# Three small moves in a fused attention and FP4 feed-forward kernel: when a scale chain runs, how a product is cut, when one GpSimd step is released

## The chip, the cores and the metric

The kernel runs on one NeuronCore of a Trainium2 chip. The metric is device time in microseconds (us) of one execution, the median of several runs. Three runs of the kernel before gave 592.62, 592.73 and 593.84 us, so the median is 592.73 us. One more execution was profiled; it took 592.31 us, and its trace spans 590.6 us from the first to the last instruction.

## The reference

`x` is 4 x 2048 x 256 in float32. Every token row is normalised, and the normalised row goes down two paths that meet in a product:

```python
xn = _layernorm(x, axis=-1)
s  = _L0_attn_ref(xn, Wq, bq, Wk, bk, Wv, bv, gamma)   # linear attention: xn + gamma * (value_sum + Q (K V)) / (L + Q sum(K))
g  = _silu(_L0_ffn_ref(xn, w_gate, w_up, w_down))      # silu(gate) * up, then down; every operand in blocks of 16 in FP4
x  = x + s * g
```

`_L0_ffn_ref` takes each operand, activations too, block by block of 16: scale = max|block| / 6, divide, round to the FP4 grid, multiply by the scale. The hidden width is 704, so gate and up together are 1408 wide.

## The kernel before

The 8192 rows are taken in 32 pairs of 128-row tiles, and an iteration `p` works on several pairs at once, a software pipeline written out by hand for each engine. In iteration p, pair p+3 is normalised and split into a float16 high part (ScalarE) and low part (`x_low`, GpSimd, L530), and its block scales are made (`x_scales`); pair p+2 is rounded to the grid (`x_round`); pair p goes through the gate and up matmuls (L1516) and the product with silu (`h_mul`, L1000); the hidden values of pair p-1 are rounded (`h_round`); pair p-2 goes through the down product; pair p-10 gets s * g (`e_half`, called y below, L1059), and pair p-12 the final sum o = y + x on GpSimd (L591). Each of PE (TensorE), DVE (VectorE), ACT (ScalarE), POOL (GpSimd) and SP (the DMA issuer) runs its own list in order, tied to the others by semaphores. Iterations 12 to 27 are two rounds of a hardware loop over batches of eight pairs, in which the values that semaphores are waited for are held in registers; the others are written out. In six of the eight positions of a batch, steps of the attention's small matrix algebra (`attention(j, c)`) lie between those of the list.

An iteration has two halves, j = 0 and j = 1, one for each tile. On VectorE the first half reads: `h_mul(0,0)`, y of columns 0 to 127, statistics of a later pair (L953, L957) and two small reciprocals and maxima (L1021, L1025), `h_mul(0,1)`, y of columns 128 to 255, the block maxima xam (`x_scales` part 0, L964), the two rounding steps xt and xg (`x_round` parts 0 and 1, L980 and L983), the low part of the hidden scales (`parts` 2, L1030, two instructions), the scale xss (part 1, L967), the low part xs2 of an earlier pair's scales (part 3, L974), the first rounding step of the hidden values (`h_round` 0, L1037), the reciprocal xrr (part 2, L971). The second half begins with `h_mul(1,0)`; in it lie `h_round` 1 (L1040), then for each tile two products hq (L1048), high part (semaphore hhiq) and low part (semaphore hloq). Between the pairs of products of tile 0 and tile 1 are `h_mul(1,1)` and a y. The maxima ham (L1007), hss (L1011) and the reciprocal hrr (L1014) end the iteration.

On GpSimd an iteration is: ht (L571, released by hrr of the iteration before), from iteration 12 on the sum o (L591), the small power steps rs and x_shift (L520, L523, released by `h_round` 0), `x_low` (L530), and the division xt of pair p+3 (`x_divide`, L537, released by the last hq). In position i = 3 of a batch a small power step (L576) stands between ht and o. The sum of pair e runs in iteration e+12.

y lives where the attention product s was left by TensorE (L1537): in columns 352 to 479 of the second bank of each of the two double banks of `GU`, 128 columns in each, beside the gate and up results. TensorE may write gate and up of the next half into a double bank when `h_mul` and y have both read it. `gate_up(p, 1, 0)` waits for y of columns 0 to 127 of the first half.

Of the kernel before, what the change touches and what calls it, by code (L numbers as in the profile page):

```python
# [29 lines left out]
P = 128  # L30
D = 256
# [9 lines left out]
CH = I // 2  # L41
# [10 lines left out]
GRING = 9  # L52
# [18 lines left out]
def build(nc, x, Wq, bq, Wk, bk, Wv, bv, gamma, w_gate, w_up, w_down, out):  # L71
# [3 lines left out]
    with ExitStack() as ctx:  # L75
# [10 lines left out]
        GU = ps("GU", [P, 2, 2, 512])  # L86
# [91 lines left out]
        unm = sb("unm", [P, 2])  # L178
# [40 lines left out]
        def wait(eng, name, value):  # L219

            if not (isinstance(value, int) and value <= 0):
                eng.wait_ge(S[name], value)
# [123 lines left out]
        def s_beside(p, j, tail):  # L346

            if tail:
                return False
            on = active(p if j else p - 1, False)  # L350
            return on["e"] and on["m"]
# [5 lines left out]
        def last_halves(j, i):  # L357

            return j == 0 and i == FIRST
# [122 lines left out]
        def _(pool):  # L482
# [75 lines left out]
            def iteration(p, k, b=0, i=-1, tail=False):  # L558
                on = active(p, tail)
                if i == 3:  # L560

                    wait(pool, "gram_d", 2 * b + 2)
                if on["mb"]:

                    u, q = p - 1, (k + 1) % 2
                    wait(pool, "hrr_d", u + 1)
                    wait(pool, "hg_d", u)
                    if isinstance(p, int) and u == 0:

                        pool.wait_ge(S["wgd"], 3)  # L570
                    g.tensor_tensor(paired(ht[:, 0:2 * I]), paired(h[:, q]), spread(hrr[:, q], 4 * CB),  # L571
                                    ALU.mult).then_inc(S["ht_d"], 1)
                last_batch = isinstance(b, int) and b == BATCHES - 1
                if i == 3 and not last_batch:
                    wait(pool, "nrm_d", b + 1)
                    g.tensor_tensor(inv[:, :], nrm[:, :], half[:, :], ALU.pow).then_inc(S["inv_d"], 1)  # L576
                if on["o"] and not (isinstance(p, int) and p - LAGO == PAIRS - 1):
                    e, ko = p - LAGO, (k + LAGO) % 2
                    wait(pool, "y_d", 4 * e + 4)
                    if isinstance(e, int) and e == PAIRS - LAGE:  # L580

                        pool.wait_ge(S["hloq"], 2 * PAIRS)
                    y_ = y_place(e) if isinstance(e, int) and e >= PAIRS - PB else y[:, ko]
                    if at_end(p):
                        pool.wait_ge(*((S["x_mid_in"], 16) if e == PAIRS - PB else (S["xend_in"], 16 * ENDS)))
                        g.tensor_tensor(end_row(p), y_, end_row(p), ALU.add).then_inc(S["o_d"], 1)
                    else:
                        wait(pool, f"xe_in{ko}", 8 * (e - ko) + 16)

                        wait(pool, f"out_d{ko}", 8 * (e - ko) + 16)  # L590
                        g.tensor_tensor(o[:, ko], y_, xe[:, ko], ALU.add).then_inc(S["o_d"], 1)  # L591
                if isinstance(p, int) and p == 0:
                    pool.wait_ge(S["dupd"], 4)
                    x_low(p, k)
                if on["xf"]:
                    if on["mb"]:

                        wait(pool, "hw_d", p)
                    x_rstd(p + 1)
                if on["xa"]:  # L600
                    if on["mb"]:

                        wait(pool, "hloq", 2 * p - 1)
                        x_low(p, k)
                    if on["mb"]:

                        wait(pool, "hloq", 2 * p)
                    else:
                        pool.wait_ge(S["h_d"], 4)
                    x_divide(p, k)  # L610
                if i == 2 and last_batch:
                    wait(pool, "nrm_d", b + 1)
                    g.tensor_tensor(inv[:, :], nrm[:, :], half[:, :], ALU.pow).then_inc(S["inv_d"], 1)
# [326 lines left out]
        def _(dve):  # L940
# [92 lines left out]
            def h_round(p, k, part):  # L1033
# [7 lines left out]
                if part >= 2:  # L1041
# [5 lines left out]
                    for at, scales, done in ((I, hs1, "hhiq"), (0, hs2, "hloq")):  # L1047
                        v.tensor_tensor(paired(hq[:, q, j, at:at + I]), paired(hg[:, j * I:(j + 1) * I]),  # L1048
                                        spread(scales[:, q, j * HB:(j + 1) * HB], HB), ALU.mult).then_inc(S[done], 1)

            def e_half(p, k, j, c, last=False):
                e, q, row = s_place(p, k, j)
                n = 4 * e + 2 * row + c
                wait(dve, "s_d", 4 * e + 4 if last else n + 1)
                wait(dve, "g_d", 2 * e + row + 1)
                if row == 0 and c == 0:

                    wait(dve, "o_d", e - 1)
                v.scalar_tensor_tensor(y[:, q, row * D + c * P:row * D + (c + 1) * P],  # L1059
                                       s_spare(0, 1 - c) if last else s_spare(c), unm[:, 0:1],  # L1060
                                       ring(gring, e, GRING)[:, row, c * P:(c + 1) * P], ALU.mult, ALU.mult).then_inc(S["y_d"], 1)
# [229 lines left out]
            def iteration(p, k, b=0, i=-1, tail=False):  # L1291
                on = active(p, tail)

                def attention(j, c):
                    step = at_step(ANSWERS, ANSWERS_END, b, (i, j, c))
                    if step == "high_low" and not (isinstance(b, int) and b == BATCHES - 1):

                        wait(dve, "y_d", 4 * b * PB)
                    if step:
                        answer(b, step)  # L1300

                if on["m"]:
                    h_mul(p, k, 0, 0, i)
                if s_beside(p, 0, tail):
                    e_half(p, k, 0, 0, last_halves(0, i))
                if s_beside(p, 0, tail) and last_halves(0, i):
                    e_half(p, k, 0, 1, True)
                attention(0, 0)
                own = on["xf"] and not (isinstance(p, int) and p == 0)
                if own:  # L1310
                    x_front(p + 1, 1 - k)
                attention(0, 5)
                if own:

                    wait(dve, "stats", dve_pairs(p + LEADA + 1))
                    wait(dve, "var_e", p + LEADA + 1)
                if on["mb"]:
                    parts(p, k, 0)
                if own:
                    x_var()  # L1320
                if on["mb"]:
                    parts(p, k, 1)
                attention(0, 1)
                if isinstance(p, int) and p == 0:
                    down_weights()
                if on["m"]:
                    h_mul(p, k, 0, 1, i)
                if s_beside(p, 0, tail) and not last_halves(0, i):
                    e_half(p, k, 0, 1)
                attention(0, 4)  # L1330
                if on["e"] and not on["m"]:
                    e_mul(p, k, 0)
                if on["xa"]:
                    x_scales(p, k, 0)
                attention(0, 2)
                if on["xb"]:
                    x_round(p, k, 0)
                    x_round(p, k, 1)
                if on["mb"]:
                    parts(p, k, 2)  # L1340
                if on["xa"]:
                    x_scales(p, k, 1)
                if on["xb"]:
                    x_scales(p - 1, 1 - k, 3)
                attention(0, 3)
                if on["mb"]:
                    h_round(p, k, 0)
                if on["xa"]:
                    x_scales(p, k, 2)
                if on["m"]:  # L1350
                    h_mul(p, k, 1, 0, i)
                if s_beside(p, 1, tail):
                    e_half(p, k, 1, 0)
                if on["xb"]:
                    x_round(p, k, 2)
                if on["mb"]:
                    h_round(p, k, 1)
                attention(1, 0)
                if on["mb"]:
                    h_round(p, k, 2)  # L1360
                if on["m"]:
                    h_mul(p, k, 1, 1, i)
                if s_beside(p, 1, tail):
                    e_half(p, k, 1, 1)
                attention(1, 1)
                if on["mb"]:
                    h_round(p, k, 3)
                if on["m"]:
                    h_scales(p, k, 0)
                if on["e"] and not on["m"]:  # L1370
                    e_mul(p, k, 1)
                attention(1, 2)
                attention(1, 3)
                if on["m"]:
                    h_scales(p, k, 1)
                    h_scales(p, k, 2)
# [419 lines left out]
```

## Time and profile before

| | |
|---|---|
| median of 3 runs | 592.73 us (592.62 to 593.84) |
| profiled execution | 592.31 us |
| its span, first to last instruction | 590.6 us |
| TensorE matmul busy | 547.1 us, 93% |
| TensorE weight load busy | 425.8 us, 72% |
| VectorE busy | 553.9 us, 94%, 1172 instructions |
| ScalarE busy | 420.2 us, 71% |
| GpSimd busy | 252.4 us, 43%, 213 instructions |
| granted TensorE clock, mean | 0.993 of full speed |

A row of a view that lists groups ends with the busy time, the mean duration of one instruction in ns, and the idle time of the engine before them with what ended it. A row of the timeline is one instruction, or several alike in sequence (x2 says two). The duration of an instruction begins while the one before it on the same engine is still draining, by 0.07 to 0.09 us, so two in sequence take less than the sum of their durations. A wait for a semaphore counts as idle time; a wait for a memory port is inside an instruction's duration, since the instruction has been issued.

### The profile page before, as it was taken

The numbers are of one execution on the slowest core, as the hardware profiler recorded it, in microseconds if no ns is written. First come the engines' busy times: TensorE is split into PE (matmuls) and PEld (weight loads), VectorE is DVE, ScalarE is ACT, GpSimd is POOL, SyncE is SP. The second block draws the span as 40 slices with busy tenths as digits, with TensorE's granted clock in tenths as the row PEclk, the third lists the DMA queues.
The fourth block names the chain that finished last, engine by engine and source line by source line (L and its number), as shares of the span: only waits on it lengthen the run. The fifth ranks groups of instructions, "written<-read, shape, count | busy, mean of one in ns | idle before, by whom it ended". The sixth has DMA issues, their size and how long they took to land. (4 is left out here: it accounts for less than half of the span.)

```text
span 590.6 us, 15231 instructions
## 1 busy us (share of the span) xinstructions
PE 547.1 (93%) x4973; PEld 425.8 (72%) x4973; DVE 553.9 (94%) x1172; ACT 420.2 (71%) x916; POOL 252.4 (43%) x213
## 2 busy tenths in 40 slices
PE   0478999999999999999999989999999999999996
PEld 0355667778787777778787757778787777778875
DVE  7998999999999999999999998999999999987783
ACT  5989888877787787767686767777677777654431
POOL 7543433333434435435544343444343554422146
PEclk9999899999999999999999999999999999999999
DMA  8010000000011001111011111110111111004124
GB/s 253 18 36 20 20 19 19 19 19 19 19 37 37 19 1 57 55 55 55 24 48 41 54 58 56 55 39 18 55 54 55 55 37 38 22 32 145 37 90 179
DMA packets 17632, 29.14 MB, mean 49 GB/s; under 512 B 2704, under 2 KB 5136, under 8 KB 17552
## 3 DMA queue, kind: packets, MB, share of 16 engines
q1 hardware_dynamic: 17552, 28.13, 14.6%
q8 instruction: 44, 0.72, 0.5%
q14 instruction: 36, 0.29, 0.2%
HBM read 19.73 MB, written 8.39 MB: 48 GB/s over the span
## 5 line engine op out<-in xcount | busy, mean ns | idle before, releaser
L1516 PE MATMUL GU<-wgu,xqT 128*128 128x352 f16 x1536 | 252.4, 315 | 3.0 <-DVE h L1000 2.6
L1516 PEld LDWEIGHTS GU<-wgu,xqT 128*128 128x128 f16 x1536 | 148.3, 99 | 76.3 <-issue 4.1
L571 POOL TENSOR_TENSOR ht<-h,hrr 128x1408 f32<-128x1408 f32 x32 | 82.9, 2590 | 80.1 <-DVE hrr L1014 78.6
L666 ACT ACTIVATE sil<-GU,wkap 128x352 f32<-128x352 f32 x128 | 70.8, 553 | 55.6 <-PE GU L1516 54.5
L1526 PE MATMUL DS<-wdT,hqT 128*128 128x256 f16 x704 | 87.3, 272 | 0.6 <-ACT hqT L673 0.6
L1000 DVE SCALAR_TENSOR_TENSOR h<-GU,wkap,sil 128x352 f32<-128x352 f32 x128 | 68.6, 536 | 12.2 <-ACT sil L666 8.4
L1048 DVE TENSOR_TENSOR hq<-hg,hs 128x704 f16<-128x704 f16 x128 | 79.1, 658 | 1.0
L530 POOL TENSOR_TENSOR xnat<-xs,xnat 128x510 f16<-128x510 f32 (+1 forms) x32 | 37.0, 1159 | 96.6 <-DVE hq L1048 81.1
L1526 PEld LDWEIGHTS DS<-wdT,hqT 128*128 128x128 f16 x704 | 66.8, 98 | 10.5 <-ACT hqT L673 0.9
L520 POOL TENSOR_TENSOR rs<-ve,half 128x2 f32<-128x2 f32 x32 | 22.9, 716 | 111.4 <-DVE ht L1037 106.6
L702 ACT ACTIVATE gring<-DS,hun 128x256 f32<-128x256 f32 (+1 forms) x64 | 29.8, 466 | 42.2 <-issue 28.5
L673 ACT COPY hqT<-TR 128x768 f16<-128x768 f16 x64 | 50.9, 796 | 8.1 <-PE TR L1478 7.1
L1037 DVE SCALAR_TENSOR_TENSOR ht<-hT,ht 128x1408 f32<-128x1408 f32 x32 | 51.8, 1617 | 1.5 <-ACT hT L715 1.5
L1528 PE MATMUL DS<-wdT,hqT 128*128 128x256 f16 x384 | 52.4, 273 | 0.0
L1040 DVE SCALAR_TENSOR_TENSOR hg<-hT,ht 128x1408 f16<-128x1408 f32 x32 | 51.7, 1617 | 0.0
L1007 DVE TENSOR_REDUCE ham<-h 128x88 f32<-128x1408 f32 x32 | 51.4, 1607 | 0.0
L1478 PE MATMUL TR<-id,hq 128*128 128x128 f16 x704 | 50.4, 221 | 1.1 <-DVE hq L1048 0.5
L1537 PE MATMUL GU<-Mx,xnT 128*128 128x128 f16 (+1 forms) x552 | 48.1, 223 | 0.2 <-DVE y L1059 0.2
L1537 PEld LDWEIGHTS GU<-Mx,xnT 128*128 (+1 forms) x552 | 39.5, 98 | 10.6 <-issue 1.0
L537 POOL TENSOR_TENSOR xt<-xs,xrr 128x512 f32<-128x512 f32 x32 | 34.7, 1083 | 27.9 <-DVE hq L1048 25.1
L1478 PEld LDWEIGHTS TR<-id,hq 128*128 128x128 f16 x704 | 43.2, 99 | 4.5 <-issue 1.9
L715 ACT ACTIVATE hT<-ht 128x1408 f32<-128x1408 f32 x32 | 43.8, 1367 | 1.9 <-POOL ht L571 1.3
(185 smaller groups left out, 969.0 us busy)
## 6 DMA issues: line engine op xcount, KB each, us to landing
xin<-in_L_attn_x SPq DMA_DIRECT2D x34, 256.0 KB, 2.9
xe<-in_L_attn_x SPq DMA_DIRECT2D x24, 256.0 KB, 2.8
out<-o SPq DMA_DIRECT2D x24, 256.0 KB, 2.0
algebra<-in_L_ffn_w_down SPq DMA_DIRECT2D x1, 704.0 KB, 6.7
gring<-in_L_ffn_w_up SPq DMA_DIRECT2D x1, 640.0 KB, 5.1
xs<-in_L_attn_x SPq DMA_DIRECT2D x2, 256.0 KB, 4.3
xt<-in_L_attn_x SPq DMA_DIRECT2D x2, 256.0 KB, 4.8
out<-xin SPq DMA_DIRECT2D x2, 256.0 KB, 2.0
```

Source lines behind the costliest of these rows:

```text
L571: g.tensor_tensor(paired(ht[:, 0:2 * I]), paired(h[:, q]), spread(hrr[:, q], 4 * CB), ALU.mult).then_inc(S["ht_d"], 1)
L666: a.activation(sil[:, c], GU[:, c, 0, 0:CH], ACT.Silu, scale=wkap[:, 0:1]).then_inc(S["sil_d"], 1)
L1000: v.scalar_tensor_tensor(h[:, k, (2 * j + c) * CH:(2 * j + c + 1) * CH], GU[:, c, 1, 0:CH], wkap[:, 0:1], sil[:, c], ALU.mult, ALU.mult).t ...
L1007: v.tensor_reduce(per_block(ham[:, :]), paired_in_order(h[:, q]), AX.X, ALU.max, apply_absolute_value=True).then_inc(S["ham_d"], 1)
L1037: v.scalar_tensor_tensor(ht[:, 0:2 * I], hT[:, 0:2 * I], CUT, ht[:, 0:2 * I], ALU.max, ALU.subtract).then_inc(S["hw_d"], 1)
L1040: v.scalar_tensor_tensor(hg[:, 0:2 * I], hT[:, 0:2 * I], CUT, ht[:, 0:2 * I], ALU.max, ALU.subtract).then_inc(S["hg_d"], 1)
L1048: v.tensor_tensor(paired(hq[:, q, j, at:at + I]), paired(hg[:, j * I:(j + 1) * I]), spread(scales[:, q, j * HB:(j + 1) * HB], HB), ALU.mul ...
L1478: last = t.transpose(TR[:, bank, zz * P:(zz + 1) * P], hq[:, q, j, z * P:(z + 1) * P], id16[:, :])
L1516: last = t.matmul(GU[:, c, m, 0:CH], xqT[:, k, j, 2 * a_ + kc], wgu[:, b_, kc, 2 * m + c], start=(z == 0 and kc == 0), stop=(z == 2 and kc ...
L1526: t.matmul(DS[:, 0:D], hqT[:, j, z], wdT[:, z], start=(z == 0), stop=False)
L1528: last = t.matmul(DS[:, 0:D], hqT[:, j, LOCH + z], wdT[:, NCH + z], start=False, stop=(z == LOCH))
L1537: last = t.matmul(bank, slot[:, j, 2 * a_ + kc], Mb[:, b_, kc, columns], start=(i == 0 and kc == 0), stop=(i == 2 and kc == KD - 1))
```

## The change

It has four parts.

- `x_low` on GpSimd waits for the first of the two products hq of tile 0 (`hhiq`) instead of the second (`hloq`).
- y of the first half (j = 0) is one instruction over 256 columns in two banks (`e_row`), at the place where the second of the two stood. The first of them is gone from its place after `h_mul(0,0)`. It raises its semaphore by 2 at its end. One iteration of each batch (`last_halves`) keeps the two.
- Where GpSimd has a sum o to make (`on["o"]`, iterations 12 on), the two rounding steps of `x_round` stand after the scale steps instead of before them.
- There, the reciprocal xrr stands before `h_round` 0 instead of after it, and `parts` 2 after the scale steps.

```diff
                     if on["mb"]:
-                        wait(pool, "hloq", 2 * p - 1)
+                        wait(pool, "hhiq", 2 * p - 1)
                         x_low(p, k)
...
+            def e_row(p, k, j):
+                e, q, row = s_place(p, k, j)
+                halves = lambda ap: ap.rearrange("p (c n) -> p c n", c=2)
+                wait(dve, "s_d", 4 * e + 2 * row + 2)
+                wait(dve, "g_d", 2 * e + row + 1)
+                v.scalar_tensor_tensor(halves(y[:, q, row * D:(row + 1) * D]), GU[:, :, 1, CH:CH + P], unm[:, 0:1],
+                                       halves(ring(gring, e, GRING)[:, row]), ALU.mult, ALU.mult).then_inc(S["y_d"], 2)
...
                 if on["m"]:
                     h_mul(p, k, 0, 0, i)
-                if s_beside(p, 0, tail):
-                    e_half(p, k, 0, 0, last_halves(0, i))
                 if s_beside(p, 0, tail) and last_halves(0, i):
+                    e_half(p, k, 0, 0, True)
                     e_half(p, k, 0, 1, True)
...
                 if s_beside(p, 0, tail) and not last_halves(0, i):
-                    e_half(p, k, 0, 1)
+                    e_row(p, k, 0)
...
                     x_scales(p, k, 0)
                 attention(0, 2)
-                if on["xb"]:
+                if on["xb"] and not on["o"]:
                     x_round(p, k, 0)
                     x_round(p, k, 1)
-                if on["mb"]:
+                if on["mb"] and not on["o"]:
                     parts(p, k, 2)
                 if on["xa"]:
                     x_scales(p, k, 1)
                 if on["xb"]:
                     x_scales(p - 1, 1 - k, 3)
+                if on["xa"] and on["o"]:
+                    x_scales(p, k, 2)
+                if on["mb"] and on["o"]:
+                    parts(p, k, 2)
+                if on["xb"] and on["o"]:
+                    x_round(p, k, 0)
+                    x_round(p, k, 1)
                 attention(0, 3)
                 if on["mb"]:
                     h_round(p, k, 0)
-                if on["xa"]:
+                if on["xa"] and not on["o"]:
                     x_scales(p, k, 2)
```

## Rows read from the trace of the kernel before

**Rows 1.** VectorE's waits from 197 to 524 us: us in total, times, longest.

```profile
DVE h L1000 <- POOL ht L571: 2.8, 1, 2.8
```

**Rows 2.** VectorE's waits over the whole span, the longest in total.

```profile
DVE h L1000 <- ACT sil L666: 8.4, 6, 2.2
```

**Rows 3.** Timeline of VectorE at the end of iteration 16, inside the hardware loop.

```profile
298.94 0.96 DVE L1048 TENSOR_TENSOR hq<-hg,hs 128x704 f16<-128x704 f16 x2
...
300.31 0.34 DVE L1059 SCALAR_TENSOR_TENSOR y<-GU,unm,gring 128x128 f32<-128x128 f32 x1
300.57 1.61 DVE L1048 TENSOR_TENSOR hq<-hg,hs 128x704 f16<-128x704 f16 x2
```

**Rows 4.** Timeline of GpSimd in the same stretch.

```profile
300.21 1.16 POOL L530 TENSOR_TENSOR xnat<-xs,xnat 128x510 f32 x1 [3.12 <-DVE hq L1048]
```

**Rows 5.** All hq products: ns min/median/max, first and last start in us.

```profile
L1048 DVE TENSOR_TENSOR hq<-hg,hs x128: 509/519/1208, 61.5 to 573.8; 128x704 f16<-128x704 f16 x128
```

**Rows 6.** Timeline of VectorE at the end of iteration 1, before the loop.

```profile
61.46 0.96 DVE L1048 TENSOR_TENSOR hq<-hg,hs 128x704 f16<-128x704 f16 x2
...
62.83 1.63 DVE L1048 TENSOR_TENSOR hq<-hg,hs 128x704 f16<-128x704 f16 x2
```

**Rows 7.** Timeline of GpSimd in the same stretch.

```profile
62.49 1.16 POOL L530 TENSOR_TENSOR xnat<-xs,xnat 128x510 f16<-128x510 f32 x1 [2.89 <-DVE hq L1048]
```

**Rows 8.** Timeline of VectorE, iteration 16, the first rounding step.

```profile
291.35 0.68 DVE L980 SCALAR_TENSOR_TENSOR xt<-xT,xt 128x512 f32<-128x512 f32 x1
```

**Rows 9.** Timeline of GpSimd there: the sum o.

```profile
291.77 1.39 POOL L591 TENSOR_TENSOR o<-y,xe 128x512 f32<-128x512 f32 x1
```

**Rows 10.** Timeline of VectorE, iteration 19: xam to the first `h_mul` of half 1.

```profile
342.83 0.67 DVE L964 TENSOR_REDUCE xam<-xs 128x32 f32<-128x512 f32 x1
343.43 1.28 DVE L980 SCALAR_TENSOR_TENSOR xt<-xT,xt 128x512 f32<-128x512 f32 x1
...
345.36 0.43 DVE L1030 SCALAR_TENSOR_TENSOR hs<-hss,hbq,hs 128x44 f16<-128x44 f32 x2
...
345.89 1.62 DVE L1037 SCALAR_TENSOR_TENSOR ht<-hT,ht 128x1408 f32<-128x1408 f32 x1
347.43 0.34 DVE L971 RECIPROCAL xrr<-xss 128x32 f32<-128x32 f32 x1
347.69 0.48 DVE L1000 SCALAR_TENSOR_TENSOR h<-GU,wkap,sil 128x352 f32<-128x352 f32 x1
```

**Rows 11.** Timeline of GpSimd there.

```profile
342.88 1.28 POOL L591 TENSOR_TENSOR o<-y,xe 128x512 f32<-128x512 f32 x1
```

**Rows 12.** The two rounding steps over the span: ns min/median/max.

```profile
L980 DVE SCALAR_TENSOR_TENSOR xt<-xT,xt x32: 679/682/1374, 30.1 to 512.8; 128x512 f32<-128x512 f32 x32
L983 DVE SCALAR_TENSOR_TENSOR xg<-xT,xt x32: 691/692/1650, 30.9 to 513.6; 128x512 f16<-128x512 f32 x32
```

**Rows 13.** The small hidden-scale step from 520 to 560 us: ns min/median/max.

```profile
L1030 DVE SCALAR_TENSOR_TENSOR hs<-hss,hbq,hs x4: 252/258/361, 529.7 to 547.1; 128x44 f16<-128x44 f32 x4
```

**Rows 14.** Timeline of GpSimd at the first of these four.

```profile
528.69 1.27 POOL L591 TENSOR_TENSOR o<-y,xe 128x512 f32<-128x512 f32 x1
```

**Rows 15.** s * g over 256 columns from one bank, grouped by form.

```profile
L1092 DVE SCALAR_TENSOR_TENSOR y<-GU,unm,gring 128x256 f32<-128x256 f32 x6 | 2.8, 479 | 0.3 <-PE GU L1537 0.3
```

**Rows 16.** Timeline of TensorE's weight loads, iteration 19: the gate and up of half 1.

```profile
340.97 1.61 PEld L1516 LDWEIGHTS GU<-wgu,xqT 128*128 128x128 f16 x12 [0.37 <-DVE y L1059]
```

**Rows 17.** Timeline of VectorE there: the second `h_mul` of half 0.

```profile
342.07 0.58 DVE L1000 SCALAR_TENSOR_TENSOR h<-GU,wkap,sil 128x352 f32<-128x352 f32 x1
```

**Rows 18.** Timeline of ScalarE: silu for `h_mul(1,0)` of iterations 19 and 17.

```profile
344.64 0.54 ACT L666 ACTIVATE sil<-GU,wkap 128x352 f32<-128x352 f32 x1
...
311.63 0.56 ACT L666 ACTIVATE sil<-GU,wkap 128x352 f32<-128x352 f32 x1 [1.76 <-PE GU L1516]
```

**Rows 19.** Timeline of VectorE: that `h_mul(1,0)` of iteration 17, and one of iteration 30.

```profile
312.98 0.48 DVE L1000 SCALAR_TENSOR_TENSOR h<-GU,wkap,sil 128x352 f32<-128x352 f32 x1
...
528.34 0.58 DVE L1000 SCALAR_TENSOR_TENSOR h<-GU,wkap,sil 128x352 f32<-128x352 f32 x1 [0.68 <-ACT sil L666]
```

## The prediction

> **What bounds the kernel now.** I read the waits first. From 197 to 524 us, iterations 11 to 29, VectorE waits for another engine once, 2.8 us [rows 1], at the turn of the hardware loop. Over the whole span its largest wait is for silu, 8.4 us in six places [rows 2]; these lie in iterations 0, 1, 30 and 31. So VectorE's own list sets the time in the middle, and a microsecond taken off it there is a microsecond, until TensorE or ScalarE is late. In iterations 8 and 9 silu comes only just in time, and from iteration 30 on TensorE has a part in the pace: in iteration 30 `h_mul` waits for silu [rows 19].
>
> A list can be full and still hold waiting. The timeline shows where. In iteration 16 the first two products hq take 0.96 us together, the next two 1.61 us [rows 3], and one alone has a median of 0.52 us but a maximum of 1.21 us [rows 5]. The long one stands beside `x_low` on GpSimd, 300.21 to 301.37 us [rows 4]. It ends 0.38 us after `x_low`, which is its 0.52 us less some 0.14 us of start: it waited inside itself. The same shows at the first rounding step: 1.28 us [rows 10] beside the sum o, which ends at 344.16 [rows 11], against a median of 0.68 [rows 12]. So a VectorE operation with two inputs in SBUF and a large GpSimd operation exclude each other. The one that is under way goes first: the rounding step at 291.35 kept its 0.68 us [rows 8] although o came at 291.77, and o took 1.39 instead of 1.28 us [rows 9, 11]. It overlapped the running step for 0.26 us and paid 0.11, so again some 0.15 us of an overlap is free.
>
> **x_low one operation sooner.** In the loop `x_low` starts 0.31 us after the second product of tile 0 ends (298.94 + 0.96 = 299.90; 300.21) [rows 3, 4]. The first ends 0.96 - 0.52 = 0.44 us before the second. Released by it, with the same 0.31 us, `x_low` starts at 299.77, beside the last 0.13 us of the second product, which is within the free 0.15. It ends at 300.93 instead of 301.37. The blocked product of tile 1, which starts at 300.57 as before, gets free 0.44 us sooner; 0.2 us of its 0.65 us (1.61 - 0.96) stay. VectorE gains 0.44 us in each of iterations 12 to 27, 16 x 0.44 = 7.0 us.
> Outside the loop `x_low` starts 0.07 us after its release [rows 6, 7]. It will start at 62.05, 0.37 us before the running product ends at 62.42, pay 0.37 - 0.15 = 0.22, and end at 63.43 instead of 63.65: 0.22 us gained. That holds in iterations 1 to 11 and 28. From about 4 to 9 I take TensorE's own list to set the pace (silu has no time in hand at 8 and 9), and what VectorE gains after iteration 28 starts its second half is lost in the wait of iteration 30. I count six, 1.3 us. GpSimd itself has over a microsecond idle ahead of `x_low` in each of these [rows 4, 7], and the step before it, x_shift, is long done.
> The bounds of this part: 0 if the lock behaves otherwise, 12 x 0.22 + 16 x 0.65 = 13 us if nothing of the blocked time stayed.
>
> **y of the first half in one operation.** A y of 128 columns adds 0.26 us to the list (300.31 to 300.57) [rows 3]. One of 256 columns lasts 0.48 us [rows 15] against 0.34, so it adds 0.26 + 0.14 = 0.40. 2 x 0.26 - 0.40 = 0.12 us less in each of 19 iterations, at most 2.3 us. Where o blocks the next step this only makes VectorE arrive sooner and wait longer, so in about half of them it is nothing.
> The price is on TensorE. Its gate and up of the second half is released by the first y now, 340.97 [rows 16]; after the change by `e_row`, which in iteration 19 would end at 342.07 + 0.50 + 0.48 = 343.05 [rows 15, 17]: 2.1 us later. Behind it in TensorE's list are s, the hidden transposes and all later gate and up. Silu for this half starts at 344.64 now [rows 18], about 2 us after the last weight load, since ScalarE is busy with other steps. With gate and up done near 345.0 it starts near 345.1 and ends near 345.7, and `h_mul(1,0)` comes at 347.69 [rows 10]: covered by 2 us. The like lag, worked out in the same way, is 0.5 to 2.2 us in iterations 11 to 14, 19, 20, 22, 27 and 28, 12.1 us together; in 15 to 17 and 23 to 25 TensorE is behind anyway and comes after the place of `e_row`. The lag lasts until TensorE's next wait for VectorE. I take 0.2 us as lost; if the cover were gone everywhere it would be the 12.1 us.
>
> **The scale steps ahead of the rounding.** In iterations 12, 13, 15, 19, 21, 23 and 27 the first rounding step waits some 0.6 us for o, as in iteration 19; in 16, 24, 28 and 29 the second waits some 0.95 us (1.65 against 0.69) [rows 12]. What takes their place right after xam? xss (one input), then xs2, a step with two SBUF inputs like the rounding. It starts where xt started: 0.12 later for xss (0.03 of gap and 0.09 of lost overlap, since xss needs xam finished), 0.1 for xss itself, 0.12 to 0.13 earlier by `e_row`, so 0.1 later. The nearest row for such a small step beside o is that of iteration 30: 361 ns instead of 256 [rows 13], beside an o that ends at 529.96 [rows 14], 0.06 us before it. So it waits too. Then after the end of o there is still all of the old work but xss: 2.0 us before (xt 0.55, xg 0.73, hs2 with xss and xs2 0.53 (345.36 to 345.89), xrr 0.26 (347.43 to 347.69)) [rows 10], 1.9 after. The gain is 0.1 us in the seven, not 0.6. In 16 and 24 hs2 would now wait for o, and both rounding steps come behind it: 0.1 lost each. In 17 and 25, where 0.15 us was lost to o, 0.1 gained. Where nothing collides the order costs the 0.12 us behind xam, which `e_row` pays (14, 20, 22) or not (18, 26: 0.1 lost each). Sum with `e_row` of iteration 11: 0.7 - 0.2 + 0.2 - 0.2 + 0.1 = 0.6. Its bounds: below, -0.12 x 17 = -2 us; above, if small steps slip past o, 7 x 0.5 + 4 x 0.2 = 4.4 us more.
> The reciprocal and hs2 move past no queue but VectorE's; the only reader of xrr, the division on GpSimd, waits for the last hq anyway. ScalarE's input of hs2 was ready before (it is made ahead of its Abs step).
> The Trainium skill, page "SBUF — State Buffer", section "Who interferes with whom", says that a VectorE instruction with two SBUF inputs contends with a GpSimd one that reads SBUF, whichever issued first blocking the other. That speaks against the reordering: xs2 and hs2 have two. The rows above agree for the long steps and, by one row, for the short. It adds tensor_scalar in its two-port modes, which would block xss too; no row here shows it, and it would make the 0.1 of the seven iterations 0.
>
> **The sum.** 7.0 + 1.3 - 0.2 + 0.6 = 8.7 us, of which I take 8.5 for what drains and waits eat. The profiled execution took 592.31 us for its 590.6, so 583.8 against its own time; the median is 0.4 above it: 584.2 us.
>
> **Rivals.**
> Small steps slip past o (0.15): for it, xss and xrr have one input and the row for hs2 is single; against it, that row. 584.2 - 4.4 = 580.
> TensorE or ScalarE takes over (0.18): in iteration 17 silu ends at 312.19 and `h_mul(1,0)` starts at 312.98 [rows 18, 19], so only 0.8 us is in hand there after two or three gains of 0.44. If iterations 15 to 18 and 23 to 26 gave nothing, 8 x 0.44 = 3.5 is lost: 588.
> No change (0.09): two thirds of the lags of `e_row`, 8 us, reach VectorE: 592.2. For it, TensorE has little idle time; against it, the covers above.
> Slower (0.08): `x_low`, now arriving while a product runs, takes the port first. Then the second product of tile 0 waits for all of `x_low` and ends at 301.3 instead of 299.90, and the list is 1.4 - 0.65 = 0.75 us longer each time: 28 x 0.75 = 21 us, or with the rest 605. It decides as soon as a GpSimd operation can pass a running VectorE one; the step at 291.35 speaks against it [rows 8]. Milder, the whole of `e_row`'s lag, 12.1 - 8.5: 596.3.
> The forecast itself has 0.50, with 582.5 to 586.5 as its own range.
>
> **How the numbers follow.** A measurement of this kernel can tell some 0.2%, 1.2 us, from no change. Faster: forecast, first and second rival, 0.83. Same 0.09, slower 0.08. The range reaches from 579.5 (small steps slip past) to 590.0 (TensorE takes over, with something of the lag).
>
> **What would show it.** `x_low` 0.4 us earlier after the first product in the loop; the third hq at 0.7 to 0.75 us there and near 0.98 outside instead of 1.2; the y of 256 columns at 0.48; xs2 or hs2 at about 0.7 us where o overlaps them, and both rounding steps at 0.68 in iteration 19. The gate and up of half 1 starts after `e_row` in iteration 19. The prediction is wrong if new waits of `h_mul` for silu appear in iterations 11 to 29, or if xs2 keeps 0.18 us beside o.

## The result, and the profile after

The changed kernel takes 588.44 us (median of 6 runs, 587.57 to 590.46) beside 593.29 us for the kernel before in the same session (6 runs): ratio 0.9926, 95% interval 0.9902 to 0.9950, so 4.4 us less by the ratio and 4.85 us by the medians. Forecast were 584.2 us, 8.5 us less. The profiled execution took 587.87 us, its trace spans 586.1 us.

Three rows of the page (the hq products beside rows 5). VectorE (DVE) is busy 543.2 us, 10.7 us less than before, and the kernel gained less than half of that:

```profile
PE 541.6 (92%) x4973; PEld 423.6 (72%) x4973; DVE 543.2 (93%) x1153; ACT 421.4 (72%) x916; POOL 245.9 (42%) x213
...
L1000 DVE SCALAR_TENSOR_TENSOR h<-GU,wkap,sil 128x352 f32<-128x352 f32 x128 | 70.5, 551 | 16.7 <-ACT sil L666 13.3
...
L1048 DVE TENSOR_TENSOR hq<-hg,hs 128x704 f16<-128x704 f16 x128 | 69.5, 583 | 1.0
```

The hq products answer to the forecast (0.7 to 0.75 us for the blocked one in the loop, near 0.98 outside: 0.72 to 0.75 and 0.98 to 0.99). Timeline of VectorE at the end of iteration 16 (as rows 3) and of iteration 1 (as rows 6):

```profile
297.64 0.96 DVE L1048 TENSOR_TENSOR hq<-hg,hs 128x704 f16<-128x704 f16 x2
...
299.27 1.17 DVE L1048 TENSOR_TENSOR hq<-hg,hs 128x704 f16<-128x704 f16 x2
```

```profile
62.09 0.96 DVE L1048 TENSOR_TENSOR hq<-hg,hs 128x704 f16<-128x704 f16 x2
...
63.46 1.42 DVE L1048 TENSOR_TENSOR hq<-hg,hs 128x704 f16<-128x704 f16 x2
```

and of GpSimd in both places (as rows 4 and 7):

```profile
298.47 1.16 POOL L530 TENSOR_TENSOR xnat<-xs,xnat 128x510 f32 x1 [2.35 <-DVE hq L1048]
```

```profile
62.69 1.38 POOL L530 TENSOR_TENSOR xnat<-xs,xnat 128x510 f16<-128x510 f32 x1 [2.46 <-DVE hq L1048]
```

In the loop the second pair takes 1.17 us instead of 1.61, in iteration 1 1.42 instead of 1.63, and there `x_low` pays 0.22 us for coming while a product runs (1.38 against 1.16).

What is new is in the waits, and it is what the prediction named as the sign of being wrong: `h_mul` waits for silu in iterations 11 to 29. VectorE, from 190 to 524 us (as rows 1; us in total, times, longest):

```profile
DVE h L1000 <- ACT sil L666: 5.3, 7, 1.7
DVE h L1000 <- POOL ht L571: 2.8, 1, 2.8
```

Of the 5.3 us 1.7 are iteration 30's, whose wait was 0.68 before (rows 19); 3.7 us have come in iterations 14, 15, 23 and 29, where there was none. TensorE's weight loads from 190 to 524 us, the first two groups by time:

```profile
PEld GU L1530 <- DVE y L1056: 3.9, 3, 1.8
PEld GU L1530 <- DVE y L1067: 2.7, 1, 2.7
```

L1056 is `e_row`. Of its nineteen instructions four are waited for: those of iterations 19 and 27 (1.81 us each) and 20 (0.33 us) make up this row, and that of iteration 11 (1.68 us) is put down to issue, though the load starts 0.1 us after `e_row` ends. The 2.7 us of the second row lie at the turn of the hardware loop, where TensorE waits in every trace here, 3.1 us in that of the kernel before. Timeline of the weight loads, iteration 11, and iteration 19 (as rows 16):

```profile
205.09 0.64 PEld L1542 LDWEIGHTS DS<-wdT,hqT 128*128 128x128 f16 x6
207.41 1.62 PEld L1530 LDWEIGHTS GU<-wgu,xqT 128*128 128x128 f16 x12 [1.68 <-issue]
```

```profile
340.52 0.71 PEld L1530 LDWEIGHTS GU<-wgu,xqT 128*128 128x128 f16 x6 [1.81 <-DVE y L1056]
```

And the sum o. Timeline of VectorE in iteration 19 after the change (as rows 10), then GpSimd (as rows 11):

```profile
340.38 0.67 DVE L964 TENSOR_REDUCE xam<-xs 128x32 f32<-128x512 f32 x1
341.09 0.77 DVE L967 TENSOR_SCALAR xss<-xam 128x32 f32<-128x32 f32 x1
341.78 0.18 DVE L974 SCALAR_TENSOR_TENSOR xs<-xss,xs 128x32 f16<-128x32 f32 x1
341.89 0.35 DVE L971 RECIPROCAL xrr<-xss 128x32 f32<-128x32 f32 x1
342.16 0.34 DVE L1030 SCALAR_TENSOR_TENSOR hs<-hss,hbq,hs 128x44 f16<-128x44 f32 x2
342.42 0.69 DVE L980 SCALAR_TENSOR_TENSOR xt<-xT,xt 128x512 f32<-128x512 f32 x1
```

```profile
340.55 1.27 POOL L591 TENSOR_TENSOR o<-y,xe 128x512 f32<-128x512 f32 x1
```

The rounding no longer waits; xss does, 0.77 us where it takes 0.18 alone, until o ends at 341.82. In iteration 16 it is hs2 that waits (1.45 us for the two instead of 0.43):

```profile
290.06 0.35 DVE L971 RECIPROCAL xrr<-xss 128x32 f32<-128x32 f32 x1
290.33 1.45 DVE L1030 SCALAR_TENSOR_TENSOR hs<-hss,hbq,hs 128x44 f16<-128x44 f32 x2
291.71 0.68 DVE L980 SCALAR_TENSOR_TENSOR xt<-xT,xt 128x512 f32<-128x512 f32 x1
```

So the open question was not where VectorE's time went but what took it back. **Theory A:** the wait that the late `e_row` puts on TensorE, handed on from iteration to iteration, since TensorE has no idle time in which to make it good, until silu is late. **Theory B:** TensorE's own work is the bound of iterations 12 to 16, and any faster VectorE would have met it.

### The profile page after: what moved, and what is told of

The parts are those of the page before. It is cut to its first block, busy times and chain, and to the rows that moved or that the text cites. A ratio compares the mean times of both kernels' runs of the same rounds, so it can differ in the third digit from the quotient of the medians.

```text
span 586.1 us, 15165 instructions
## 1 busy us (share of the span) xinstructions
PE 541.6 (92%) x4973; PEld 423.6 (72%) x4973; DVE 543.2 (93%) x1153; ACT 421.4 (72%) x916; POOL 245.9 (42%) x213
## 4 chain that ended last, share of the span: by engine, by line
PE 74%; DVE 12%; issue 6%; ACT 4%; POOL 2%; DMA 1%; SPq 0%; DVEq 0%; ACTq 0%; POOLq 0%
PE GU L1530 32%; PE DS L1540 11%; PE GU L1551 6%; PE DS L1542 6%; PE TR L1492 6%; PE G L1600 4%; PE TR L1508 2%; DVE hg L1040 2%; PE TR L1432 2%; DVE ham L1007 2%; DVE hq L1048 1%; DVE h L1000 1%; PE G L1615 1%; PE G L1641 1%; DMA gring<-in_L_ffn_w_up 1%
## 5 line engine op out<-in xcount | busy, mean ns | idle before, releaser
L1000 DVE SCALAR_TENSOR_TENSOR h<-GU,wkap,sil 128x352 f32<-128x352 f32 x128 | 70.5, 551 | 16.7 <-ACT sil L666 13.3
L530 POOL TENSOR_TENSOR xnat<-xs,xnat 128x510 f16<-128x510 f32 (+1 forms) x32 | 39.6, 1238 | 90.7 <-DVE hq L1048 81.9
L1048 DVE TENSOR_TENSOR hq<-hg,hs 128x704 f16<-128x704 f16 x128 | 69.5, 583 | 1.0
L675 ACT COPY hqT<-TR 128x640 f16<-128x640 f16 x64 | 45.0, 702 | 0.0
```

The source lines that it names most:

```text
L1000: v.scalar_tensor_tensor(h[:, k, (2 * j + c) * CH:(2 * j + c + 1) * CH], GU[:, c, 1, 0:CH], wkap[:, 0:1], sil[:, c], ALU.mult, ALU.mult).t ...
```

## The experiments

e1 to e4 were timed beside the kernel before in one session, e5 to e8 in another on another chip; the kernel before took 592.42 and 592.46 us there. A time is a median; the ratio goes by all runs of a session, and the two can differ by some 0.6 us where the runs of a kernel scatter, as those of e3 to e5 do (586.5 to 589.2 us).

**e1: x_low alone.** The edit against the kernel before:

```diff
-                        wait(pool, "hloq", 2 * p - 1)
+                        wait(pool, "hhiq", 2 * p - 1)
```

> The kernel before with the one edit on GpSimd: x_low released by the first product hq of tile 0. Theory A (the lag that the 256-column y puts on TensorE took the missing gain): without that y TensorE keeps its lead, VectorE's 0.44 us in each loop iteration come through, and the time is 8.0 us under the kernel before, near 585.0 us beside its 593.3; silu waits between 197 and 524 us under 1 us in total. Theory B (TensorE's own work is the bound in iterations 12 to 16, whoever releases it): the same 588.4 us as the changed kernel, silu waits of 4 to 5 us in that stretch, in iterations 15 and 23.

584.72 us, ratio 0.9875 (0.9860 to 0.9890): 7.7 us faster than before, and 3.6 us faster than e4 below (3.0 us by the ratios). VectorE's waits from 190 to 524 us:

```profile
DVE h L1000 <- issue: 3.2, 3, 2.5
...
DVE h L1000 <- ACT sil L666: 0.7, 1, 0.7
```

The 3.2 us are the turn of the loop, 2.5 us, and 0.37 us each in iterations 14 and 22, which the kernel before has too. The 0.7 us is the wait of iteration 30 (rows 19), which now falls into this stretch. Theory B had the same 588.4 us here; it falls. TensorE's weight loads in iteration 11 of e1 go on without a break:

```profile
204.72 0.64 PEld L1528 LDWEIGHTS DS<-wdT,hqT 128*128 128x128 f16 x6
205.37 1.70 PEld L1516 LDWEIGHTS GU<-wgu,xqT 128*128 128x128 f16 x12
```

**e2: the changed kernel without the 256-column y.** Against the changed kernel:

```diff
+                if s_beside(p, 0, tail):
+                    e_half(p, k, 0, 0, last_halves(0, i))
                 if s_beside(p, 0, tail) and last_halves(0, i):
-                    e_half(p, k, 0, 0, True)
                     e_half(p, k, 0, 1, True)
...
-                    e_row(p, k, 0)
+                    e_half(p, k, 0, 1)
```

> The changed kernel with y of the first half in two operations at their old places; x_low and the order as changed. Theory A: 1.5 to 3 us faster than the changed kernel, 585.5 to 587 us, with the waits for silu in iterations 15 and 23 (0.9 and 0.7 us for the second h_mul there now) gone. Theory B: within 0.7 us of the changed kernel, 588 to 589 us, since the waits stay.

586.58 us, ratio 0.9902 (0.9887 to 0.9917), inside A's range though near its slow end. The waits in 15 and 23 are gone, but it is 1.9 us slower than e1, from which it differs by the new order alone: the order costs (1.6 us by the ratios).

**e3: the changed kernel with the old order** (the guards `and not on["o"]` and the second block with `on["o"]` taken out).

> The changed kernel with the old order of scale steps and rounding; x_low and the 256-column y as changed. The trace after shows the wait for the sum o moved from the rounding steps to xss (0.77 us instead of 0.18), hs2 and xs2 and as long as before, so both theories expect the same: 588.4 us, within 1 us of the changed kernel. If the order is worth more than that, the time is 590 us or more.

587.28 us, ratio 0.9911 (0.9897 to 0.9926). The changed kernel was timed in a session of its own; in the ratio, the one measure that the sessions share, e3 is 0.0015 under it, with intervals that overlap: no difference that this measurement can tell. Why the order doesn't show beside the late y was not tested; that VectorE waits for silu there anyway would explain it.

**e4: two y of 128 columns, both at the late place**, with `x_low` as changed and the old order. The y against the changed kernel:

```diff
                 if s_beside(p, 0, tail) and not last_halves(0, i):
-                    e_row(p, k, 0)
+                    e_half(p, k, 0, 0)
+                    e_half(p, k, 0, 1)
```

> x_low as changed, old order, and y of the first half in its two old operations, but both at the late place, after the second h_mul: the lag of TensorE without the shorter y. Theory A: the loss comes with the place, so 588.5 to 590 us, the changed kernel or a little slower (19 x 0.12 us more on VectorE, where it has no waits). Theory B: as e1, 588.4 us; the two theories are told apart by e1 against e4, which A has 3.5 to 5 us apart and B under 1 us.

588.33 us, ratio 0.9926 (0.9912 to 0.9939), within 0.2 us of A's range, and 3.6 us from e1 (3.0 by the ratios) where B had them together. The loss is there with two instructions of the old length: it is the place of the first y, not its form.

**e5: the 256-column y in one position of eight.** `joined` chooses `e_row`; elsewhere the two `e_half` stand at their old places. Against the kernel before, `x_low` left out:

```diff
-                if s_beside(p, 0, tail):
+                joined = i == 6
+                if s_beside(p, 0, tail) and not joined:
                     e_half(p, k, 0, 0, last_halves(0, i))
...
-                    e_half(p, k, 0, 1)
+                    if joined:
+                        e_row(p, k, 0)
+                    else:
+                        e_half(p, k, 0, 1)
```

> x_low as changed, old order, and the 256-column y in position i = 6 of a batch alone (iterations 11, 19 and 27), the two old ones everywhere else. In the trace after, TensorE waits for the 256-column y 1.7 to 1.8 us in these three iterations and runs back to back from there to iteration 15 or 23, 2.0 us later than in e1 all the way. If one such wait per batch is the whole cause, this kernel loses nearly all that e3 and e4 lose: 587.3 to 588.5 us, with waits for silu in iterations 15 and 23. If each late y adds its own part, three of nineteen cost little: 585 to 585.7 us.

588.68 us, ratio 0.9926 (0.9911 to 0.9940), 0.2 us past the expected range: three late y lose as much as nineteen. TensorE's weight loads in iteration 11, and VectorE in iteration 15, 64 us later:

```profile
204.86 0.64 PEld L1540 LDWEIGHTS DS<-wdT,hqT 128*128 128x128 f16 x6
207.19 0.87 PEld L1528 LDWEIGHTS GU<-wgu,xqT 128*128 128x128 f16 x7 [1.68 <-issue]
```

```profile
271.06 0.58 DVE L1000 SCALAR_TENSOR_TENSOR h<-GU,wkap,sil 128x352 f32<-128x352 f32 x1 [0.79 <-ACT sil L666]
...
276.84 0.58 DVE L1000 SCALAR_TENSOR_TENSOR h<-GU,wkap,sil 128x352 f32<-128x352 f32 x1 [0.36 <-ACT sil L666]
```

The y of iterations 12 to 15 stand in their old places here, and VectorE waits all the same: 1.68 us of idle TensorE in iteration 11 come out as 0.79 + 0.36 us of idle VectorE in iteration 15. In the changed kernel the same two waits are 0.94 and 0.39 us.

**e6: the 256-column y where TensorE comes late anyway**, `joined = i in (2, 3, 4)`.

> The complement where TensorE comes late anyway: x_low as changed, old order, the 256-column y in positions i = 2, 3 and 4 alone (iterations 15 to 17, 23 to 25, 31), where in e1 its gate and up of the second half starts 1.4 to 2.7 us after the second h_mul, past the end of the 256-column y. No new wait on TensorE; VectorE has 6 x 0.12 = 0.7 us less to do, of which what falls in iterations 17 and 25 is lost to silu: 584.0 to 584.8 us, e1 or up to 0.5 us faster. If the 256-column y costs anything besides its place, it is 586 us or more.

584.89 us, ratio 0.9871 (0.9857 to 0.9885), 0.1 us past the expected range: e1 and e6 cannot be told apart. Where the gate and up starts after the place of `e_row` anyway, the 256-column y costs nothing, and its gain is too small to see.

**e7: the 256-column y alone**, GpSimd and order as before.

> The kernel before with the 256-column y alone, GpSimd and the order as before. VectorE is shorter by some 17 x 0.12 = 2.0 us. If the place costs only what exceeds silu's cover, then with VectorE slower by 0.44 us an iteration than in e3 the cover at iterations 15 and 23 is near 1.1 us against a lag of 1.9, and 0.8 us is lost per batch, some at 29: within 0.8 us of the kernel before, 591.8 to 593.2. If the lag reaches VectorE whole, 595 us and more; if it were free, 590.4.

592.28 us, ratio 0.9995 (0.9984 to 1.0005): no change. Its waits for silu between 190 and 524 us, all up to iteration 29, are 1.9 us, against 3.7 in the changed kernel up to there. With a slower VectorE silu's cover, the time from its end to its `h_mul`, is wider.

**e8: the order alone.**

> The kernel before with the new order alone. The order moves the wait for the sum o from the rounding to xss and adds the drain between xam and xss: from e2 against e1 +0.15 us in iterations without a collision, +0.2 in iterations 16, 18, 24 and 26, +0.03 in the others, 1.2 to 1.9 us in total: 593.6 to 594.4 us beside 592.4. If the order pays on its own as it was costed in the prediction, 592.0 us.

594.15 us, ratio 1.0026 (1.0016 to 1.0036): 1.7 us slower (1.5 by the ratio). Its xss, and that of the kernel before, ns min/median/max:

```profile
L967 DVE TENSOR_SCALAR xss<-xam x29: 171/180/750, 46.0 to 498.5; 128x32 f32<-128x32 f32 x29
```

```profile
L967 DVE TENSOR_SCALAR xss<-xam x29: 166/173/176, 46.1 to 499.9; 128x32 f32<-128x32 f32 x29
```

**Where each kernel is ahead.** From the timelines: the start of `h_mul(0,0)` of an iteration, less that of the kernel before, in us, both counted from iteration 1 (which takes out differences of -0.06 to 0.63 us that arise before it); the last column is the end of the span.

| iteration | 7 | 8 | 12 | 15 | 16 | 20 | 23 | 24 | 29 | 31 | end |
|---|---|---|---|---|---|---|---|---|---|---|---|
| e1 x_low alone | -1.29 | -0.67 | -1.09 | -2.42 | -2.85 | -4.58 | -5.86 | -6.30 | -7.97 | -7.94 | -7.95 |
| e2 x_low, order | -1.28 | -0.67 | -1.07 | -2.17 | -2.57 | -3.88 | -4.46 | -4.88 | -6.46 | -6.33 | -6.33 |
| changed kernel | -1.29 | -0.68 | -1.22 | -2.63 | -2.13 | -3.38 | -4.93 | -4.70 | -6.26 | -5.05 | -5.05 |
| e3 x_low, wide y | -1.30 | -0.68 | -1.22 | -2.73 | -2.12 | -3.80 | -4.26 | -3.68 | -5.29 | -4.16 | -4.16 |
| e5 wide y at i = 6 | -1.33 | -0.69 | -1.24 | -2.75 | -2.14 | -3.77 | -4.21 | -3.62 | -5.19 | -4.05 | -4.06 |
| e8 order alone | 0.00 | -0.02 | -0.02 | 0.17 | 0.20 | 0.31 | 1.02 | 1.03 | 1.34 | 1.44 | 1.44 |

Read the row of e1: 0.22 us an iteration to the seventh, 0.6 us given back in iteration 7 to TensorE, then 0.42 to 0.45 us in most iterations of the loop. The rows with the late y go with it to 15, or up to 0.3 us ahead; all three lose 0.5 to 0.6 us in iteration 15 where e1 gains 0.43, and 1.1 to 1.2 us in 29 and 30 together. In 23 the changed kernel loses 0.2 us, e3 and e5 0.6, and these two also 0.4 in 22. They agree within 0.11 us in every column.

**TensorE's clock at the turn of the loop.** The wait of iteration 22 is in the traces of e3, e4 and e5, 1.0 to 1.2 us, and not in that of the changed kernel. TensorE's granted clock differs. The stretches around its start after the turn, in e3 and in the changed kernel (the number after the five engines is the granted clock; a row has no engine names, and they stand in the order PE, PEld, DVE, ACT, POOL):

```profile
347.40:350.40 3.00, 1.00 (x6) 0.27 (x4) 2.97 (x7) 0.47 (x1) 1.79 (x2) 1.00 0.03 8
350.40:354.40 4.00, 4.00 (x28) 3.00 (x29) 2.85 (x4) 2.41 (x5) 1.99 (x2) 0.65 0.03 8
```

```profile
348.00:351.00 3.00, 0.75 (x5) 0.14 (x4) 2.97 (x7) 0.57 (x2) 1.15 (x1) 1.00 0.01 3
351.00:355.00 4.00, 4.00 (x38) 2.97 (x39) 2.59 (x4) 3.52 (x7) 2.24 (x2) 1.00 0.03 8
```

In e3 the clock is at the lower of its two levels (1.2 of 2.4 GHz) for most of 4 us, and 28 matmuls are done instead of 38. From the first half's gate and up to the second's, iteration 20 takes 9.6 us instead of 7.9. The traces of the kernel before, e2, e4, e5 and e8 have this, those of the changed kernel, e1, e6 and e7 do not have it there; TensorE was nearly idle before it in all of them (e1: 0.61 us busy of the last 3, full clock after). Where the y is not late VectorE had the time in hand: e2 has no wait in 22. Beside the late y its 1.7 us come on top of the lag:

```profile
391.32 0.58 DVE L1000 SCALAR_TENSOR_TENSOR h<-GU,wkap,sil 128x352 f32<-128x352 f32 x1 [1.17 <-ACT sil L666]
```

is e3 in iteration 22. The runs' times fit this, though they are few. A run with a mean granted clock of 0.999 or 1.0 has no such stretch, since one takes 0.0024 off the mean (0.35 x 4 of 587 us): these took 586.58 and 587.28 us for e3 and 587.12 for e4, against 584.64 for e1. Runs at 0.993 and 0.994 took 588.0 to 589.2 us for e4 and e5. Runs at 0.997 have one such stretch, and only a trace tells where. The changed kernel is less clear: its three runs at 0.999 took 587.57, 587.83 and 589.01 us.

## Why the prediction was wrong

**x_low: right, in mechanism and size.** The forecast for this edit was 7.0 + 1.3 = 8.3 us; e1 measures 7.7 (7.4 by the ratio, 7.95 in the table). In the loop 1.61 - 1.17 = 0.44 us were gained as worked out, outside 1.63 - 1.42 = 0.21 for 0.22, and the price of 0.22 us for an arrival during a running product is the row's 1.38 - 1.16. The iterations outside the loop came to 1.1 us at iteration 12 (the table), and 28 adds 0.2: the 1.3 that was put. The loop brings 6.7 us for 7.0: iterations 17 and 25 gain only 0.17 and 0.15 us, as silu has nothing in hand any more there, and 19 gains 0.71, as the wait at the turn of the loop is 0.28 us shorter (2.50 for 2.78), a wait that is 2.50 to 2.80 us in the ten traces. The rival in which GpSimd passes a running product is excluded by the same rows.

**The 256-column y: the step that failed.** The prediction had the lag of TensorE right (2.1 us in iteration 19; the weight loads start at 340.52, 0.06 us after `e_row` ends at 340.46, and 1.81 us idle) and set it against silu's time in hand at the next `h_mul`: "covered by 2 us". There it was covered. But it also wrote that the lag lasts until TensorE's next wait for VectorE, and did not look for that wait. In e1 it comes in the second half of iteration 15, 0.76 us; with the late y it is gone, used up by the lag. From iteration 11 to there TensorE's gate and up keep their distance to e1, 1.6 us counted as in the table (1.8 to 2.0 us from the start of the traces), with no idle time to make it good. The lag has to be held against the thinnest cover on that way. Silu and its `h_mul` in e1, of the two of iteration 15 that wait in e5 and in the changed kernel:

```profile
268.76 0.56 ACT L666 ACTIVATE sil<-GU,wkap 128x352 f32<-128x352 f32 x1 [0.83 <-PE GU L1516]
...
274.53 0.55 ACT L666 ACTIVATE sil<-GU,wkap 128x352 f32<-128x352 f32 x1 [1.22 <-PE GU L1516]
```

```profile
270.44 0.58 DVE L1000 SCALAR_TENSOR_TENSOR h<-GU,wkap,sil 128x352 f32<-128x352 f32 x1
...
276.05 0.48 DVE L1000 SCALAR_TENSOR_TENSOR h<-GU,wkap,sil 128x352 f32<-128x352 f32 x1
```

Silu ends 1.1 and 1.0 us before them, less than the lag. So a term of 0.2 us for lost cover measured 2.6 us (e3 against e1) to 4.0 us (e5 against e1) by the medians, 2.1 to 3.0 by the ratios; in the three runs without the lower clock it is 1.9 to 2.6 us, and where that clock meets the lag, the wait of iteration 22 comes on top. The reckoning of lags one by one, 12.1 us together, was the wrong shape: the late y of iterations 11, 19 and 27 give the whole loss, as e5 shows, and those after them fall into their shadow. This was the rival "TensorE or ScalarE takes over", whose 588 us is what was measured, but its reason was another: it named the 0.8 us in hand at iteration 17, with the gains of `x_low` alone as the cause, and in e1 that cost only some 0.3 us each time. That its number fits is luck.
That the two edits work against each other shows in the sums: the y alone changes nothing (e7, -0.2 us), `x_low` alone brings 7.7, together 5.1 (e3). A faster VectorE uses up the cover that the lag needs.

**The order: the wait moved as predicted, its cost was missed.** Forecast was that a small step with two SBUF inputs waits for o, so that the reordering saves nothing of the 0.6 us. That held: hs2 waits in iteration 16. What the sum missed is that xss, with one input, waits too; the prediction had no row for it and named it only as a possibility, with this result. With it the 0.1 us gained in seven iterations is 0.0, and e2 lies 0.02 to 0.05 us behind e1 in each of 12, 13, 15, 21 and 23. The drain between xam and xss, put at 0.12 us, measured 0.14 to 0.16 where nothing collides (14, 18, 22, 26), and the 0.1 us lost in 16 and 24 was 0.19. Iterations 19 and 20 add 0.8 us between e2 and e1. 0.23 of it is the wait at the turn, 2.74 us against 2.50, which varies from trace to trace (2.52 in e8) and can't be laid to the order. In iteration 20 e2 and e8 both lose 0.5 us: the 0.15 behind xam, 0.29 us for which VectorE stands idle before xrr, put down to issue, which neither e1 nor the changed kernel has, and the overlap lost with it. Why it stands there is open. Together 1.7 us (e8) to 1.9 us (e2 against e1) are lost by the medians. The 0.6 us of the prediction was for the order and the shorter y together: 0.12 of it is iteration 11's, and 0.36 is what the shorter y pays in iterations 14, 20 and 22, so 0.1 us was put for the order alone. In the changed kernel the loss does not show in the time (e3).
The rule of the Trainium skill, "SBUF — State Buffer", "Who interferes with whom", that a tensor_scalar in a two-port mode contends with GpSimd, agrees with the trace: xss takes 0.77 us instead of 0.18 beside o. The trace shows the wait, not the mode.

**The sum.** 8.3 + 0.6 - 0.2 = 8.7 was written and taken as 8.5. The measured pieces by the medians are 7.7 for `x_low`, -2.6 for the late y beside it, and -0.3 for the order beside both, which makes the 4.8 measured; by the ratios 7.4, -2.1 and -0.9, which makes 4.4. The last piece lies within the scatter either way. The range, 579.5 to 590, held the time; the size was missed by almost half.

**The better version.** `x_low` alone, e1, 584.72 us, is 7.7 us faster than the kernel before and, by the ratios 0.9875 and 0.9926, some 3 us faster than the changed one; e6 is as good. e3 and e5, which have the old order, show 0.9 to 1.0 us less gain than the changed kernel at the end of the span in the table. Their traces have the lower clock at the turn and the changed kernel's has not, and the traced run of e3 took 588.58 us, 1.3 above its median, so the table doesn't show that the order helps. What stays open: whether it helps or costs a little beside the late y, and what decides in a given run whether the clock falls at the turn.

## What to carry to other kernels

When an edit makes a producer later, follow the delay along its own list to the next place where it waits, and compare it with the thinnest cover on the whole way, not with the cover next to it; an engine without idle time hands a delay on for several iterations, and here the later delays that fell inside the first one added nothing. When two edits are bundled, ask whether one consumes the slack that the other needs. A wait for a shared port does not go away by putting small instructions first: look in the trace for the very form of instruction beside the very partner, before it is taken to be free. And when two traces are compared, compare the granted clock in the same places too: an engine's slack may cover a stretch of lower clock in one kernel and not in the other.

## What the runs showed of the hardware

A VectorE tensor_scalar on 128x32 float32, SBUF to SBUF, takes 0.18 us alone and waits for a GpSimd tensor_tensor that is under way (0.77 to 0.87 us in iterations 12, 13, 19, 21 and 27 of the changed kernel, ending 0.04 us after it). A reciprocal of the same size beside the sum o (iteration 28) takes 0.35 us, as alone. The prediction had left both open. That a GpSimd tensor_tensor which arrives during a two-input VectorE operation never overtakes it held in every one of the 28 places: the second hq took 0.52 us in each. After 2.5 to 3.1 us without weight loads at the turn of the loop, TensorE's granted clock fell to 0.5 for a few microseconds in six of ten traces and not in the other four.
